# The last 64 keys of two heads in one score tile, and key 1600 as side work: two layers of cross-attention on one core

## The reference

```python
x = x + L0_xattn(layernorm(x), ctx, ctx)     # q, k, v, softmax(q k / 4) v, projection
x = x + L0_ffn(layernorm(x))                 # 2 shared and 8 routed experts, 2 of 8 per token
x = x + L1_xattn(layernorm(x), ctx, ctx)
x = x + L1_ffn(x)                            # sqrt((x cos t)^2 + (x sin p)^2)
```

## Time and profile before

| what | value |
|---|---|
| median of three runs | 1292.52 us |
| the profiled execution | 1293.05 us |
| its span | 1291.3 us |
| TensorE, share of the span busy | 91% |
| ScalarE | 80% |
| VectorE | 53% |
| GpSimd | 13% |
| first layer's units | 49.86 to 437.00 us |
| experts | 437.00 to 866.00 us |
| second layer's units | 866.00 to 1259.20 us |

### The profile page before, as it was taken

The page is one execution under the profiler, slowest core; times in us unless marked ns, Lnnn a source line. Parts: engine busy times, 40 slices in busy tenths (PEclk is TensorE's granted clock), DMA queues, the critical chain, the costliest instruction groups (busy, mean ns, idle before and its releaser), DMA issues. The chain is left out here.

```text
span 1291.3 us, 43625 instructions
## 1 busy us (share of the span) xinstructions
PE 1171.7 (91%) x17942; PEld 579.3 (45%) x17942; DVE 681.2 (53%) x1622; ACT 1038.0 (80%) x1482; POOL 174.3 (13%) x211
## 2 busy tenths in 40 slices
PE   8888898898898999999999999978989999998995
PEld 5322232232222356677999998742223223222222
DVE  5224757757646576554666666643335433333335
ACT  4599999999999854443666666549999999999992
POOL 5111211111010020333000010223220000000000
PEclk9999999999999999999999999989999999999997
DMA  7236735535637243211443454222120000010001
GB/s 200 63 122 200 257 100 161 180 100 160 204 99 223 88 125 101 95 61 50 118 134 112 117 152 131 73 81 80 41 61 10 24 23 2 20 27 3 2 3 65
DMA packets 106305, 124.94 MB, mean 97 GB/s; under 512 B 25091, under 2 KB 89310, under 8 KB 106142
## 3 DMA queue, kind: packets, MB, share of 16 engines
q1 hardware_dynamic: 89088, 85.95, 21.7%
q0 software_dynamic: 9328, 29.37, 7.2%
q10 hardware_dynamic: 7726, 7.26, 1.9%
HBM read 70.27 MB, written 46.95 MB: 91 GB/s over the span
## 5 line engine op out<-in xcount | busy, mean ns | idle before, releaser
L888 ACT ACTIVATE prob<-banks 128x1024 f32<-128x1024 f32 (+1 forms) x832 | 771.8, 1052 | 8.1 <-PE banks L1679 4.5
L1694 PE MATMUL banks<-prob,v 64*32 64x512 f32 x6656 | 442.6, 593 | 0.6 <-ACT prob L888 0.6
L1679 PE MATMUL banks<-zone,kst 52*32 52x512 f16 x6528 | 337.6, 385 | 85.5 <-ACT prob L888 79.8
L1679 PEld LDWEIGHTS banks<-zone,kst 52*32 52x32 f16 x6528 | 92.7, 89 | 493.8 <-ACT prob L888 479.0
L1694 PEld LDWEIGHTS banks<-prob,v 64*32 64x32 f32 x6656 | 118.7, 106 | 21.6 <-ACT prob L888 2.4
L2327 PE MATMUL banks<-xsT_d,w 128*128 128x128 f16 x1776 | 123.6, 219 | 2.1 <-issue 1.2
L2327 PEld LDWEIGHTS banks<-xsT_d,w 128*128 128x128 f16 x1776 | 108.6, 98 | 10.9 <-issue 7.7
L2338 PE MATMUL banks<-w,hh 128*128 128x256 f16 x592 | 107.0, 273 | 0.0
L2124 DVE TENSOR_TENSOR hl<-hid,hh 128x128 f16<-128x128 f32 x296 | 83.2, 291 | 30.4 <-ACT hh L2051 22.3
L2047 ACT ACTIVATE hid<-banks,b 128x128 f32<-128x128 f32 x222 | 74.5, 369 | 25.0 <-PE banks L2327 20.6
L2290 PE MATMUL banks<-w,hh 128*128 128x256 f16 x480 | 80.6, 276 | 2.0 <-DVE outb_d L2209 2.0
(11 more groups left out here) (275 smaller groups left out, 1285.2 us busy)
## 6 DMA issues: line engine op xcount, KB each, us to landing
weight_parts<-late SPq DMA_DIRECT2D x54, 256.0 KB, 3.8
w<-weight_parts POOLq DMA_DIRECT2D x24, 512.0 KB, 3.9
late<-in_L_ffn_W_r SPq DMA_DIRECT2D x43, 256.0 KB, 4.2
weight_parts<-more SPq DMA_DIRECT2D x26, 256.0 KB, 3.1
zone<-q_parts SPq DMA_DIRECT2D x180, 32.0 KB
slot_rows<-late POOLq DMA_DIRECT2D x14, 384.0 KB, 4.2
more<-in_L_ffn_W_r SPq DMA_DIRECT2D x21, 256.0 KB, 3.9
xs_d<-slot_rows ACTq DMA_DIRECT2D x39, 128.0 KB, 2.1
```

What stands on the lines that cost most here:

```text
L888: nc.scalar.activation(prob[0:m, t % P_RING, 2 * (n % 2):2 * (n % 2) + 2, :], score[G % S_RING][0:m, :, :], ACT.Exp, scale=0.25).then_inc( ...
L1679: last = nc.tensor.matmul(score[G % S_RING][j:j + wide, a, :], kst[stack, 2 * q + n % 2, t * P + j:t * P + j + wide], qst[stack, u % Q_RIN ...
L1694: last = nc.tensor.matmul(outp[u % 2][GROUP * j:GROUP * (j + 1), a, :], v[rows, t, u % NQ, j, :], prob[rows, (u * KT + t) % P_RING, j, :], ...
```

## The change

The last tile of 65 keys is divided. Its first 64 keys are made for two heads at a time in one tile of 128 partitions, the second head's in the upper half (`packed_half`): a unit has 25 groups of scores (`PAIRS`), and the values of these 64 keys are projected into both halves. The one key that is left, number 1600, becomes a side piece of its own, `last`: TensorE computes its scores for the four heads, repeated over 32 partitions (`last_scores`), VectorE transposes the bank into SBUF in blocks of 32 (`take_last`), ScalarE takes one exponential of 128x16 after the first of the next unit (`last_exponentials`), VectorE spreads it by a second transpose (`spread_last`) and adds it, times the value of key 1600, when it finishes the unit. That value is made once for each layer by 32 one-column products (`project_last_value`, `last_values`). GpSimd no longer writes zeros and ones for the last tile.

```diff
-PAIRS = 2 * KT
+PAIRS = 2 * (KT - 1) + 1
+PACKED = PAIRS - 1
...
+LAST_AT = ((4, 11, 10, 8), (5, 8, 5, 11))
+FIRST_LAST_AT = ((8, 11, 10, 8), (5, 11, 10, 6))
...
-                nc.gpsimd.memset(v[HALF:P, KT - 1], 0.0).then_inc(v_cleared, 1)
-                for b in range(2):
-                    pool.wait_ge(v_cleared, 3 + b)
-                    nc.gpsimd.memset(beside(b)[HALF:KLAST, KT - 1:KT], 1.0).then_inc(v_cleared, 1)
-                pool.wait_ge(v_cleared, 5)
...
+            def last_exponentials(u):
+                act.wait_ge(side_free, at["last", u // NQ, u % NQ] + 1)
+                nc.scalar.activation(lastexp[:], turned_last(u).rearrange("p (n r) -> p n r", r=GROUP)[:, :, 0], ACT.Exp, scale=0.25).then_inc(last_exp, 1)
...
+                    if u and n == 0:
+                        last_exponentials(u - 1)
+            last_exponentials(UNITS - 1)
...
+            def take_last(u):
+                bank = take("last", u // NQ, u % NQ)
+                if u == 0:
+                    dve.wait_ge(mask_stored, 64)
+                nc.vector.transpose(turned_last(u), bank).then_inc(side_free, 1)
+            def spread_last(u):
+                dve.wait_ge(last_exp, u + 1)
+                nc.vector.transpose(osum, lastexp[:].unsqueeze(2).broadcast_to([P, CH // GROUP, GROUP])).then_inc(last_spread, 1)
+                dve.wait_ge(last_spread, u + 1)
...
+                spread_last(u)
                 dve.wait_ge(pv_done, KT * (u + 1))
-                nc.vector.tensor_copy(osum, outp[u % 2][:, 0, :]).then_inc(half_read, 1)
+                nc.vector.scalar_tensor_tensor(osum, osum, vlast[:, i, b:b + 1], outp[u % 2][:, 0, :],
+                                               ALU.mult, ALU.add).then_inc(half_read, 1)
...
                     else:
                         cuts(u, 1, 2)
+                    take_last(u)
                     if done:
                         out_normalise(c - 1)
                     cuts(u, 2, CUTS)
...
                     if done:
                         take_turned(c - 1, 0)
                         take_turned(c - 1, 1)
+                    take_last(u)
                     cuts(u, 3, CUTS)
...
                     if done:
                         for i in range(1, TPC):
                             take_wave(c - 1, i)
+                    take_last(u)
...
+            def project_last_value():
+                for i in range(DH):
+                    for b in range(2):
+                        for j in range(QH):
+                            n0 = i * P + b * HALF + (j - b) * HD
+                            for c in range(DH):
+                                last = nc.tensor.matmul(lastp[GROUP * j:GROUP * (j + 1), i, b:b + 1], wv[:, c, n0:n0 + GROUP],
+                                                        g.ctxT[:, c, KV - 1:KV], start=(c == 0), stop=(c == DH - 1),
+                                                        tile_position=(0, GROUP * j))
+                last.then_inc(last_projected, 1)
...
+                    for k in range(0, HALF, GROUP):
+                        for j in range(QH):
+                            a, i = j % 2, j // 2
+                            stack, row = slice(HALF * a, HALF * a + STACK), HALF * packed_half(j) + k
+                            last = nc.tensor.matmul(score[G % S_RING][row:row + GROUP, i, :], kst[stack, 2 * q + i, t * P + k:t * P + k + GROUP],
+                                                    qst[stack, u % Q_RING, i, :], start=True, stop=True,
+                                                    tile_position=(HALF * a, row))
...
+            def last_scores(c, q):
+                u = NQ * c + q
+                bank = begin("last", c, q)
+                for j in range(QH):
+                    a, i = j % 2, j // 2
+                    stack = slice(HALF * a, HALF * a + STACK)
+                    last = nc.tensor.matmul(bank[GROUP * j:GROUP * (j + 1), :], kst[stack, 2 * q + i, KV - 1:KV].broadcast_to([STACK, GROUP]),
+                                            qst[stack, u % Q_RING, i, :], start=True, stop=True, tile_position=(HALF * a, GROUP * j))
+                last.then_inc(side_done, 1)
```

More of the change, by code:

```diff
@@ L123, in side_pieces @@
         back = [("xturn", c - 1, 0), ("xturn", c - 1, 1)] if done else []
+        lasts = [[("last", c, q)] if c < NC else [] for q in range(NQ)]
+        waves = [("wave", c - 1, i) for i in range(TPC)] if done else []
         if layer == 0:
-            order += outs + turns + asked[:1] + back + asked[1:] + ([("logit", c - 1, 0)] if done else [])
-        else:
-            order += turns + outs if c >= 1 else outs + turns
-            order += asked + back + ([("wave", c - 1, i) for i in range(TPC)] if done else [])
+            order += lasts[0] + outs + turns + lasts[1] + asked[:1] + back + lasts[2]
+            order += asked[1:] + ([("logit", c - 1, 0)] if done else []) + lasts[3]
+        elif c == 0:
+            order += lasts[0] + turns + lasts[1] + asked + lasts[2] + lasts[3]
+        else:
+            order += turns + lasts[0] + outs + lasts[1] + asked[:1]
+            order += asked[1:] + lasts[2] + back + waves + lasts[3]
     return {name: n for n, name in enumerate(order)}
@@ L887, in _ @@
                         act.wait_ge(pv_done, t - P_RING + 1)
-                    nc.scalar.activation(prob[0:m, t % P_RING, 2 * (n % 2):2 * (n % 2) + 2, :],
-                                         score[G % S_RING][0:m, :, :], ACT.Exp, scale=0.25).then_inc(exp_done, 1)
+                    nc.scalar.activation(prob[:, t % P_RING, 2 * (n % 2):2 * (n % 2) + 2, :],
+                                         score[G % S_RING], ACT.Exp, scale=0.25).then_inc(exp_done, 1)
+                    if u and n == 0:
+                        last_exponentials(u - 1)
+            last_exponentials(UNITS - 1)
             if first:
@@ L1054, in first_preparations @@
                     low_part(*name)
-                for _, o, n in bounds:
+                for i, (_, o, n) in enumerate(bounds):
                     bound_product(o, n)
+                    if i == 2:
+                        last_values()
                     if n == len(BCH) - 1:
@@ L1575, in project_values @@
             def project_values(t):
-                m = m_of(t)
                 if t >= 2:
@@ L1674, in scores @@
                         pe.wait_ge(k_loaded[q], 16 * K_LOADS)
-                for j in range(0, m, GROUP):
-                    wide = min(GROUP, m - j)
-                    for a in range(2):
-                        stack = slice(HALF * a, HALF * a + STACK)
-                        last = nc.tensor.matmul(score[G % S_RING][j:j + wide, a, :], kst[stack, 2 * q + n % 2, t * P + j:t * P + j + wide],
-                                                qst[stack, u % Q_RING, n % 2, :], start=True, stop=True,
-                                                tile_position=(HALF * a, j))
@@ L1682, in scores @@
-                last.then_inc(scores_done, 1)
+                if n < PACKED:
+                    for j in range(0, P, GROUP):
+                        for a in range(2):
+                            stack = slice(HALF * a, HALF * a + STACK)
+                            last = nc.tensor.matmul(score[G % S_RING][j:j + GROUP, a, :], kst[stack, 2 * q + n % 2, t * P + j:t * P + j + GROUP],
+                                                    qst[stack, u % Q_RING, n % 2, :], start=True, stop=True,
+                                                    tile_position=(HALF * a, j))
+                else:
+                    for k in range(0, HALF, GROUP):
[5 more added lines that the diff above has]
+                                                    tile_position=(HALF * a, row))
@@ L1693, in outputs @@
                     for j in range(QH):
+                        if t == KT - 1 and a != packed_half(j):
+                            continue
                         last = nc.tensor.matmul(outp[u % 2][GROUP * j:GROUP * (j + 1), a, :], v[rows, t, u % NQ, j, :],
-                                                prob[rows, (u * KT + t) % P_RING, j, :], start=(t == 0), stop=(t == KT - 1),
+                                                prob[rows, (u * KT + t) % P_RING, j if t < KT - 1 else j // 2, :],
+                                                start=(t == 0), stop=(t == last_tile(a, j)),
                                                 tile_position=(HALF * a, GROUP * j))
@@ L1775, in plan @@
                     pieces, times = ([], turns, asked, [])[q], LATE_AT[q]
-                elif not done or q == 0:
+                elif not done or q == 0 or (q == 2 and not first):
                     times = times[len(times) - len(pieces):]
-                return {t: piece for t, piece in zip(times, pieces)}
+                return {(LAST_AT if done else FIRST_LAST_AT)[layer][q]: ("last", c, q), **{t: piece for t, piece in zip(times, pieces)}}
             def side(name, c, *at_piece):
+                if name == "last":
```

(1 more changed line is left out.)

73 lines of the change are left out of this document (57 added, 16 removed).

## The result

The changed kernel takes **1282.03 us** (median; 1281.43 to 1288.16), the kernel before 1292.52: a ratio of 0.9928, 95% interval 0.991 to 0.9946. The forecast was 1283, with faster at 0.85.

What follows compares the result with a forecast made beforehand. ScalarE's exponentials were taken as the bound. Gain -24.8, crowding +1.8, late finishing +8.4, clock +3.1, small exponential's wait +0.6 and preparation +1.2 sum to -9.7 from 1293.05 us: 1283.3, say 1283 us; range 1271 to 1290.

Steps and rivals of the forecast that it cites:

- The bound and the gain of an exponential: ScalarE bounds the units; each loses a 0.91 us exponential and gains a 0.11 one: 31 x 0.80 = -24.8 us.
- Crowding (+1.8): TensorE, nine second-layer units: key 1600's side piece between other pieces costs 0.2 us each, +1.8 us.
- Late finishing (+8.4): Units 6, 10, 14: TensorE's side piece in tile 2 waits 2.8 us for VectorE's late finishing: +8.4 us.
- the clock (+3.1): TensorE's clock falls to 1.2 GHz behind the waits in units 6, 10, 14: 3 x 1.05, +3.1 us.
- The last unit gives nothing: Final unit: VectorE's taking and spreading of key 1600 lead to 1260.3, finishing starts at 1260.46 already: no gain.
- The small exponential's wait in units 24 and 28: Key 1600 comes after the waves in units 23 and 27; ScalarE waits some 0.3 us in the next: +0.6 us.
- Preparation (+1.2): Both layers' preparation: one-column products +1.1 each, clears -0.9 in layer two, last value tile 0.5 each: +1.2 us.
- That finishing isn't late: Rival: TensorE never waits for VectorE's finishing, so the terms 8.4 and 3.1 go: 1272 us, chance 0.25.
- The slower case: VectorE late in all nine layer-one units with a side piece in tile 2, cuts waiting for transfers: 1306 us, chance 0.07.
- Its own range: The main forecast's range, with a clock that stays and with twice the crowding: 1278 to 1288 us.
- its signs: Right if 800 large and 32 small exponentials, units 23.0 to 23.7 us, but 6, 10, 14 near 27 with tile-2 waits.
- a sign of being wrong: TensorE waiting for VectorE at tiles other than tile 2, where the side piece's wait was forecast.

Runs made afterwards that it cites:

- experiment 7: All work on key 1600 left out (output lacks it), against the kernel with one cut moved ahead of key 1600 (1271.24 us): 1267.52 us, ratio 0.9804.
- experiment 2: In units 5, 9 and 13 one of the two cuts behind key 1600 goes ahead of it, against the changed kernel: 1271.24 us, ratio 0.9833.
- (3): GpSimd's conversion and subtraction of normalised rows wait until the next finish has read the accumulators, against the changed kernel: 1273.03 us, ratio 0.9845.
- (6): In units 2, 6, 10 and 14 TensorE's side pieces move to tiles 4, 6, 8, 9 from 2, 4, 6, 8, against the changed kernel: 1274.33 us.
- experiment 5: In layer two's preparation GpSimd again clears the last tile of values in three pieces and ScalarE waits, against the changed kernel: 1282.99 us, ratio 0.9929.
- experiment 4: ScalarE does the 128x16 exponential twice in each unit, first into a spare tensor, against the changed kernel: 1284.90 us, ratio 0.9937.
- experiment 1: Key 1600 issued in tile 7 instead of 11 in units 5, 9, 13, taken before the two transposed tiles, against the changed kernel: 1272.70 us.
- 8: One cut moved from unit 2 to 3, key 1600 to tile 8 in layer two's fourth units, against the 1271.24 us kernel with one cut ahead: 1270.57 us.

## Why the prediction was right

- **The bound and the gain of an exponential.** ScalarE was the bound, and what it lost the kernel gained. A unit was to give 0.80 us; the 27 ordinary ones gave 0.72, with the small exponential at 0.12 where 0.11 stood. With no work on key 1600 at all (experiment 7) they gave 0.80, where 0.91 stood for the exponential alone: its removal was priced too high, and why a unit gives 0.1 less stays open.
- **Crowding (+1.8) was mis-sized: it cost nothing.** The ordinary units of layer two gave as much (0.72) as those of layer one (0.72). Without the late finishing the units were to give 24.8 - 1.8 - 0.6 = 22.4; they gave 11.1 with it (0.11 lost in layer one, 11.22 won in layer two), and 22.3 without it in experiment 2 (10.87 and 11.39). Of that 0.5 is unit 31's, which does not reach the end (below). Two errors stood against each other, 0.08 a unit too much gain (2.5 in all) and crowding that did not come, so that 1283 lies so near to 1282.03 is in part luck.
- **Late finishing (+8.4) and the clock (+3.1).** The place, the chain and the sizes came out as worked out: the add at 9.1 us into the unit, wanted at 6.2, a wait of 2.76 to 2.89 (9.1 less 6.2 is 2.9; the sum wrote 2.8). Three runs show it from three sides: less in VectorE's queue (2), the same queue without GpSimd beside it (3), the same lateness with nobody waiting (6). The sum was 11.5, and so was the cost in units 6, 10 and 14. But the clock's part went differently: it fell behind two of three waits, and cost some 1.4 rather than 1.05 each, so this agreement is luck in part too. (Unit 10 lasts 27.54; in experiment 5, with the same wait of 2.77 and the clock at 1.00, 26.18.)
- **The last unit gives nothing.** It even lost 0.44 us: from unit 31's start to finishing it takes 26.77 us (1223.11 to 1249.88), against 26.33 before (1234.13 to 1260.46). The chain is the one that the prediction gave (taking at 1248.12, spread at 1249.13).
- **The small exponential's wait in units 24 and 28:** 0.35 each for 0.3; the wait itself, 0.23, is ended by VectorE's transpose.
- **Preparation (+1.2): not settled.** 64 products are recorded for the 32 one-column ones, in 1.2 us with a gap of 0.2, so 1.1 was right for these products themselves. What the sum left out is the clock behind them in layer two, which stayed at 1.00 in the changed kernel's profiled execution and fell in seven others (last section). And the first exponential started at 49.42 to 51.44 us of the span in the eight kernels that prepare layer one as the changed kernel does, and the stretch between the layers took 428.87 to 432.05 in the seven that also prepare layer two so. Terms of 1 us can't be read there; the sum of both, 1.2 forecast, was -0.4 in the two executions compared (+1.4 and -1.8).
- **Rivals.** That finishing isn't late was wrong, though a single cut's place decides it: experiment 2 gives 1271.2 and that case was priced at 1272. The slower case was a real mechanism at the wrong strength. It appears in one place: at the end of unit 2 the cuts behind key 1600 wait for their transfers, the add ends late in unit 3, and TensorE's piece in tile 6 waits 0.21 us for it. Unit 3 takes 23.54 us, 0.28 more than in experiments 3 and 5, where the same code ran without that wait; in experiment 2 the wait was 0.61 and the unit 23.94. VectorE's timeline there, against the earlier trace rows:

```profile
121.34 0.71 DVE L1210 STREAM_TRANSPOSE late<-banks 128x512 f32<-128x512 f32 x1
123.65 0.49 DVE L1246 TENSOR_SCALAR more<-more,gains 128x512 f16<-128x512 f32 x1 [1.61 <-DMA more<-in_L_ffn_W_s]
...
126.24 0.49 DVE L1246 TENSOR_SCALAR late<-late,gains 128x512 f16<-128x512 f32 x1 [1.32 <-DMA late<-in_L_ffn_W_s]
...
128.52 0.49 DVE L1246 TENSOR_SCALAR late<-late,gains 128x512 f16<-128x512 f32 x1 [1.00 <-DMA late<-in_L_ffn_W_s]
```

Taking key 1600 ahead of those cuts spared it the wait, as the change says. In units 5, 9 and 13 it was taken ahead of cuts whose data were there, behind a product that was not: that order made VectorE idle with work in hand, for 1.49 us in units 5 and 9.

By the Trainium skill's figures (ScalarE: Activation LUTs, What ACT_TABLE_LOAD costs) an overlapped activation of 16 elements costs an estimated 0.106 us; the trace shows 0.12 to 0.13, near enough that the choice between the two made no difference.

Two more readings of the forecast need a word. Its own range, 1278 to 1288, is wider than the conditions named with it: a clock that stays gives 1280.2 and twice the crowding 1285.1, and the ends need no crowding at the lower one and twice the clock's cost at the upper. And of its signs, the counts of exponentials (800 and 32) and the waits in units 6, 10 and 14 came, but nine other units lasted over 23.7 us (0, 16, 21, 23 to 25, 27, 28 and 31, up to 24.51), and the wait of 0.21 us in unit 3 had been listed as a sign of being wrong.

## What to carry to other kernels

When a piece is added to an in-order queue, price what stands behind it by following that queue to the next instruction that another engine waits for, and compare that time with the time at which it is wanted: 0.9 us of reserve was all there was here, and the loss was 11.5 us in three units. Before placing the taking of a late result, fill the wait with work whose inputs are there already; one cut moved ahead raised the gain from 0.72% to 1.67%. And look for what the other engines run beside the delayed stretch: 2.5 of the 4.9 us that the cuts took were GpSimd's doing.

## What the runs showed of the hardware that was not expected

**The same wait of TensorE lowered its clock in one execution and not in another.** Nine waits of 2.65 to 2.89 us at the same places in three kernels: the clock fell behind units 6 and 10 in the changed kernel, behind 6 and 14 in experiments 4 and 5, and stayed at 1.00 behind the third in each. (Experiment 5 has the changed kernel's code in layer one.) In experiment 4, behind the waits of units 10 and 14 (columns as above):

```profile
300.60:303.80 3.20, 3.08 (x59) 0.95 (x59) 3.03 (x5) 1.86 (x2) 0.00 (x0) 1.00 0.36 116
397.55:400.75 3.20, 3.15 (x44) 1.38 (x52) 3.06 (x5) 1.02 (x1) 0.00 (x0) 0.62 0.41 119
```

So in units 10 and 14 neither the unit nor its work decides it, nor the wait's length within these bounds; what does stays open. The Trainium skill (TensorE: Matmul & The Clock Gate, Part 1: The HAM clock gate) says that the watch on TensorE's activity runs free of the kernel, so that the point of a change differs from run to run; six in nine agrees with that, though no run here shows the watch itself. Behind the 0.70 us in unit 6 of experiment 1 the clock stayed at 1.00. For a sum, such a drop is a chance, here six in nine, and some 1.4 us each time, with one exception: in unit 6 of experiment 4 the clock was 0.52 from 201.05 to 207.48, and the unit took 29.00 us, against 26.17 for unit 10 of the same execution, whose clock stayed.

**The clock fell behind the one-column products, with no long wait before it.** In the second layer's preparation the 32 one-column products of the value of key 1600 keep TensorE busy for 1.1 us, with one gap of 0.3 us or less among them, and eight value products follow at once. In the profiled execution of the changed kernel these eight took 1.96 us at a granted clock of 1.00. In those of experiments 1 to 6 and 8 they took 3.05 to 3.66 us, at 0.50 to 0.63 over the first 3 us. The two kernels without one-column products, the one before and experiment 7, took 1.99 us at 1.00. So it happened in seven of eight executions with these products and in neither of the two without. What it cost the kernel can't be read, since the stretch between the layers varies by more, and no run here shows which property of the products lowers the clock.
